# A fused tower of convolution, attention and a mixture of experts: one VectorE instruction per expert in place of two

## The chip, the cores and the metric

The kernel runs on one core of one Trainium2 chip. All data are float32. The metric is the device time of one execution in microseconds (us); before the change the median of three runs is 431.23 us (430.74 to 431.54). All numbers below are of the kernel before the change.

## What is computed

Eight samples pass one after the other through three blocks. Each has 750 frames of 64 channels; the convolution leaves 735 tokens.

```
h = conv1d(x, w_eff)                        # 16 taps, w_eff = cos(phase) w_real - sin(phase) w_imag
h = h + softmax(q k^T / 8) n                # n = layernorm(h), q = n Wq^T, k = n Wk^T, values are n
n = layernorm(h)
top two of 16 gate logits n @ gate_w + gate_b, softmax over the two
moe = sum over the chosen experts of gate * (relu(n @ w1[e] + b1[e]) @ w2[e] + b2[e])
h = h + layernorm(n + moe) * gamma + beta
```

The experts' hidden layer is 128 wide. The kernel computes all 16 experts for all tokens, and multiplies the hidden layer by a gate that is zero for experts that a token didn't choose.

## The kernel before, in words

**Tiling.** The 735 tokens are padded to 736 and lie in the free dimension, as two halves of 368 columns (HALF, line 32). A float32 matmul output of 368 columns fits in one PSUM bank; 736 don't. So each product that covers all tokens is made as two matmul groups, one for each half, into two banks.

**Streams.** Five instruction streams are written out by hand, one for each engine, with a `pipeline` that is the same for all: an opening, then passes i = 1 to 8. Pass i works on the attention of sample i, the mixture of sample i-1 (called m), the first layer norm and the score maxima of sample i+1, and the convolution of sample i+2. Passes 1 to 5 have all of these; pass 6 has no convolution; pass 7 has neither convolution nor score maxima; pass 8 is the mixture of the last sample alone (`last_mixture`). Nothing is scheduled by a tool: the order in each stream is that of the code, and semaphores tie the streams together.

**The mixture, expert by expert.** For expert e, TensorE runs `first_layer(m, e)` (L1043): for each half two matmuls, with the high and the low part of w1, into that half's bank, `up[0]` or `up[1]`. Each half's second matmul raises `s_up` by one. Then one of two ways follows:

- 13 of the 16 experts: VectorE's `hide` (L776) does bias, rectifier and gate of one half in one instruction (the larger of up and -b1, times the gate; the constant part is added by other matmuls), writes `hidden`, and raises `s_hid` by one. There are two for each expert.
- experts 10, 13 and 14 (`POOLED`, L43): ScalarE does bias and rectifier (`rectify`, L523), GpSimd the gate (`gate_hidden`, L295).

Then TensorE runs `second_layer(m, e)` (L1055), later in its stream: two matmuls that add into the bank `mix`. It waits until both halves of `hidden` are there. `hidden` has room for four experts.

**Who may write `up` again.** In passes 1 to 7 all experts use the same two banks. `first_layer` of expert e waits for each half separately until the same half of expert e-1 was read: the first half needs `s_hid` at the count that the first `hide` of e-1 gives, the second half that of the second `hide`. In pass 8 the experts rotate through three pairs of banks (`up_of`, L289: `up`, `wide0`, `wide1`) and wait for expert e-3.

**Order around the change on TensorE** (L1090 to L1190), with what stands between two first layers: 0, transposes and four score products of the attention (scores 0 and 1), 1, biases, second layer 0 and scores 2, 2, scores 3, 3, second layers 1 and 2, values and scores 4, 4, scores 5, 5, second layers 3 and 4 and values, 6, transposes of the next sample, 7, second layers 5 and 6, values and the projection, 8, three short matmuls of the attention, 9, second layers 7 and 8 and score maximum 0, 10, score maxima 1 and 2, 11, second layer 9 and a part of the convolution, 12, six transposes, 13, score maximum 3, gate logits, second layers and convolution, 14, gate transposes and score maximum 4, 15, the rest.

**Order on VectorE** (L793 to L836): the experts' `hide` pairs in order, and between them, for the next layer norm: `centre` before 0, `normalise` after 4, `keys_lo` after 7, `scale_attention` and `centre_sum` after 8, `query_lo` and `reduce_max` 0 after 9, `reduce_max` 1 and 2 before 11, `normalise` after 11, `x2_lo` and `reduce_max` 3 after 12, the top two, the gate and `reduce_max` 4 before 15.

**SyncE** sends the gates of the next sample to memory and back, as 16 broadcasts to `gates_all`, one for each expert; each waits until the expert's old gates were read (`s_hid` after both halves).

Of the kernel before, what the change touches and what calls it, by code (L numbers as in the profile page):

```python
# [25 lines left out]
ALU = mybir.AluOpType  # L26
ACT = mybir.ActivationFunctionType
# [4 lines left out]
HALF = (TOK + 1) // 2  # L32
TOKP = 2 * HALF
P = 128
# [6 lines left out]
CHUNKS = TAPS // 2  # L41
E, F = 16, 128
POOLED = (10, 13, 14)  # L43
HIDDEN = 4
CONV_CUTS = (0, 3, 5, CHUNKS)
# [3 lines left out]
BANK = 512  # L49
# [41 lines left out]
def build(nc, x_t, w_real, w_imag, phases, wq, wk, gate_w, gate_b, w1, b1_t, w2, b2, gamma, beta, out):  # L91
    ctx = ExitStack()
    with ctx:
        def sb(name, shape, dt=F32):
            return ctx.enter_context(nc.sbuf_tensor(name, shape, dt))

        def ps(name, shape):
            return ctx.enter_context(nc.psum_tensor(name, shape, F32))

        def sem(name):  # L100
            return ctx.enter_context(nc.semaphore(name))
# [16 lines left out]
        b1_neg = sb("b1_neg", [P, E])  # L118
        b1_pos = sb("b1_pos", [P, E])
# [14 lines left out]
        conv_t = sb("conv_t", [P, HALFP])  # L134
# [14 lines left out]
        x2 = [sb(f"x2_{k}", [P, TOKP + PAD], F32R) for k in range(2)]  # L149
# [10 lines left out]
        gates_all = sb("gates_all", [P, E, TOKP])  # L160
# [4 lines left out]
        relu = sb("relu", [P, 2, 2, HALF])  # L165
        hidden = sb("hidden", [P, HIDDEN, 2, HALF])
# [13 lines left out]

        wide = [ps(f"wide{k}", [P, 2, BANK]) for k in range(2)]
        small = ps("small", [P, BANK])
        up = [ps(f"up{k}", [P, BANK]) for k in range(2)]
        mix = ps("mix", [P, BANK])

        at = wide[1][:, 1, 0:2 * NT].rearrange("p (t k) -> p t k", k=2)
# [27 lines left out]
        s_ht = sem("h_transposed")  # L214
# [44 lines left out]
        s_gall = [sem(f"gates_of_expert{e}_broadcast") for e in range(E)]  # L259
        s_bmm = sem("bias_added")  # L260
        s_up = sem("up_ready")
        s_hid = sem("hidden_ready")
        s_relu = sem("relu_done")
        s_phid = sem("pooled_hidden_ready")
        s_down = sem("down_done")
# [19 lines left out]
        def split(ap):  # L285

            return ap.rearrange("p (s n) -> p s n", s=2)

        def up_of(e, tail):  # L289

            if not tail or e % 3 == 0:
                return up[0][:, 0:HALF], up[1][:, 0:HALF]
            return wide[e % 3 - 1][:, 0, 0:HALF], wide[e % 3 - 1][:, 1, 0:HALF]

        def gate_hidden(eng, n, e):  # L295

# [170 lines left out]
        def _(act):  # L467
            def copy(dst, src, scale=1.0):
                return act.activation(dst, src, ACT.Copy, scale=scale)  # L469
# [7 lines left out]
            def conv_copy(n, src=small):  # L477
                act.wait_ge(s_conv, n + 1)
                act.wait_ge(s_ht, n)
                copy(conv_t[:, 0:HALF], src[:, 0:HALF]).then_inc(s_convc, 1)  # L480
# [5 lines left out]
            def h0_copy(n, buf, src=small):  # L486
                act.wait_ge(s_ht, n + 1)
                tokens_copy(h0[buf], s_h0, src)
# [15 lines left out]
            def keys_hi_again(n):  # L504
                copy(split(keys1[0:D, :]), wide[1][0:D, :, 0:HALF]).then_inc(s_kone, 1)
# [17 lines left out]
            def rectify(n, e, tail):  # L523

                k = POOLED.index(e)
                for s in range(2):
                    act.wait_ge(s_up, 2 * E * n + 2 * e + s + 1)
                    if s == 0:
                        used = hidden_before(n, POOLED[k - 2], 1, True) if k >= 2 else hidden_before(n, e, -1, True)
                        act.wait_ge(s_phid, CREDIT + used)  # L530
                    act.activation(relu[:, k % 2, s, :], up_of(e, tail)[s], ACT.Relu, bias=b1_pos[:, e:e + 1]).then_inc(s_relu, 1)  # L531

            def exponentials(i, first, end):
                for t in range(first, end):
# [29 lines left out]
            def opening():  # L564

                shift(0)
                exponentials(0, 0, 4)
                conv_copy(1, up[0])
                exponentials(0, 4, NT)
                h0_copy(1, 1, up[1])  # L570
                variance(0, cen0[1], 1)
                attention_copy(0)
                variance(1, cen1, 0)
                keys_hi(1)
                keys_hi_again(1)
                query_hi(1)
                x2_hi(0, 0)
                exp_gap(0)
                gates_to_rows(0, False)
                conv_copy(2, up[0])  # L580
                act.wait_ge(s_h1, 1)
                h0_copy(2, 0, up[1])

            def iteration(i, par, first, att, conv, ahead):
                if att:
# [45 lines left out]
        def _(dve):  # L631
# [141 lines left out]
                dve.wait_ge(s_gate, g + 8)  # L773
                dve.tensor_tensor(gates[:], pick[:, 0, :, :], second, ALU.add).then_inc(s_gates, 1)

            def hide(n, e, s, tail):  # L776

                dve.wait_ge(s_up, 2 * E * n + 2 * e + s + 1)
                if s == 0:
                    dve.wait_ge(s_gall[e], 16 * (n + 1))  # L780
                    dve.wait_ge(s_down, HIDDEN + E * n + e - HIDDEN + 1)
                dve.scalar_tensor_tensor(hidden[:, e % HIDDEN, s, :], up_of(e, tail)[s], b1_neg[:, e:e + 1],  # L782
                                         gates_all[:, e, s * HALF:(s + 1) * HALF],
                                         ALU.max, ALU.mult).then_inc(s_hid, 1)

            def hide_both(n, e, att):
                if e not in POOLED:
                    hide(n, e, 0, not att)
                    hide(n, e, 1, not att)
                elif not att:  # L790
                    gate_hidden(dve, n, e)

# [85 lines left out]
        def _(pe):  # L878
# [6 lines left out]
            def convolve(n, par, first, end, dst=small):  # L885
                if first == 0:
                    pe.wait_ge(s_x[par], 8 * (n - par) + 16)
                for k in range(first, end):
                    for s in range(2):
                        a = s * HALF + 2 * k  # L890
                        last = mm(dst[s * D:(s + 1) * D, 0:HALF], conv_w[:, k, :], xt[par][:, a:a + HALF],
                                  k == 0, k == CHUNKS - 1)
                if end == CHUNKS:
                    last.then_inc(s_conv, 1)

            def to_tokens(src, done, dst=small):

                for j in range(BLOCKS):
                    last = pe.transpose(dst[:, j * P:(j + 1) * P], src[:, j * P:(j + 1) * P], ident[:])  # L899
                last.then_inc(done, 1)  # L900
# [142 lines left out]
            def first_layer(n, e, buf, tail=False):  # L1043

                used = e - 3 if tail else e - 1
                for s in range(2):
                    if used >= 0 and used in POOLED:
                        pe.wait_ge(s_relu, hidden_before(n, used, s, True))
                    elif used >= 0:
                        pe.wait_ge(s_hid, hidden_before(n, used, s, False))  # L1050
                    dst, rhs = up_of(e, tail)[s], x2[buf][:, s * HALF:(s + 1) * HALF]
                    mm(dst, w1_hi[:, e, :], rhs, True, False)
                    mm(dst, w1_lo[:, e, :], rhs, False, True).then_inc(s_up, 1)

# [137 lines left out]
            def opening():  # L1192


                for t in range(NT):
                    max_scores(0, t, 1 - t % 2, t - 1)
                    keep_awake(2)
                pe.wait_ge(s_moe_in, 16 * MOE_LOADS)
                transpose_max(0)
                for k in range(3):  # L1200
                    convolve(1, 1, CONV_CUTS[k], CONV_CUTS[k + 1], up[0])
                    scores(0, 2 * k)
                    scores(0, 2 * k + 1)
                pe.wait_ge(s_convc, 2)
                to_tokens(conv_t, s_ht, up[1])
                for t in range(NT):
                    weigh_values(0, t, 0)
                keep_awake(1)
                attention_to_tokens(0)
                keep_awake(2)  # L1210
                pe.wait_ge(s_attn, 1)
                keep_awake(4)
                pe.wait_ge(s_h0, 2)
                pe.wait_ge(s_ln[0], 2)
                to_features(wide[1], xn1[1], s_t1)
                keep_awake(3)
                pe.wait_ge(s_khi, 2)
                keep_awake(3)
                project(1)
                pe.wait_ge(s_ln[1], 1)  # L1220
                pe.wait_ge(s_kone, 2)
                to_features(wide[1], xn2[0], s_t2)
                convolve(2, 0, 0, 1, up[0])
                gate_logits(0, 0)
                convolve(2, 0, 1, 4, up[0])
                bias_product()
                max_scores(1, 0, 0, 0)
                transpose_gates(0)
                convolve(2, 0, 4, CHUNKS, up[0])
                pe.wait_ge(s_gtc, 1)  # L1230
                for t in range(1, NT):
                    max_scores(1, t, t % 2, t - 1)
                pe.wait_ge(s_convc, 3)
                to_tokens(conv_t, s_ht, up[1])
                pe.wait_ge(s_h0, 3)

            pipeline(pe, opening, iteration)
# [37 lines left out]
```

## Time and profile before

| | |
|---|---|
| median of three runs | 431.23 us |
| profiled execution, its own time | 430.75 us |
| its span, first to last instruction | 428.8 us |
| TensorE matmul busy | 397.3 us, 93% |
| VectorE busy | 252.4 us, 59% |
| ScalarE busy | 157.8 us, 37% |
| GpSimd busy | 129.6 us, 30% |
| mean granted TensorE clock | 0.988 of 2.4 GHz |

The profiled execution took 1.95 us more than its span; what lies around the span is the start and the end of the program. A row of the timeline or of the page counts an engine as busy from an instruction's start to its end. Matmuls overlap in their pipeline: each of 368 columns is shown for 0.33 us while the next starts 0.17 us after it. VectorE's records overlap a little too: a new instruction starts before the record of the one before it ends. "PEld" is TensorE's loading of weights, which runs ahead of its matmul; a wait of TensorE is mostly shown there. "Idle before" is time in which the engine stood still, and after it stands what released it.

### The profile page before, as it was taken

Reading aid. Unit: us, or ns where it says so; the run is one execution under the profiler, and the core shown is the slowest. Engines: PE = TensorE matmul, PEld = TensorE weight load, DVE = VectorE, ACT = ScalarE, POOL = GpSimd, SP = SyncE. Lnnn points to the kernel's source line nnn. Section 1 sums busy time; section 2 is a strip of 40 time slices with the busy share of each in tenths; the row PEclk is TensorE's granted clock in tenths of the full one; section 3 lists DMA queues with packets and bytes.
Section 4 is the critical chain, followed back from the end, with each engine's and each line's share of the span. In section 5 each row is a group of like instructions: output and inputs, shape, how many; then the busy total and the mean of one; then the engine's idle time right before and its main releaser. Section 6 shows DMA issues by size and latency. Waiting matters only on the chain.

```text
span 428.8 us, 6480 instructions
## 1 busy us (share of the span) xinstructions
PE 397.3 (93%) x2326; PEld 255.4 (60%) x2326; DVE 252.4 (59%) x607; ACT 157.8 (37%) x486; POOL 129.6 (30%) x158
## 2 busy tenths in 40 slices
PE   8889887999999999999999999999999889988892
PEld 6676554766576656666575657665666556555450
DVE  3273556458745775458545874478555964464772
ACT  1346412433263325433354335341553333232121
POOL 3100300104323442146125432244215620553601
PEclk9999969999999999999999999999999999999998
DMA  6500004910096004900194007700292019401940
GB/s 184 136 0 2 1 2 150 415 39 0 8 337 262 18 2 189 409 26 2 58 393 170 5 4 289 311 20 0 73 412 104 0 39 375 174 3 41 373 174 18
DMA packets 22847, 55.93 MB, mean 130 GB/s; under 512 B 3744, under 2 KB 4768, under 8 KB 22688
## 3 DMA queue, kind: packets, MB, share of 16 engines
q1 hardware_dynamic: 22816, 55.53, 34.4%
q8 instruction: 18, 0.29, 0.3%
q14 instruction: 13, 0.11, 0.1%
HBM read 53.57 MB, written 1.95 MB: 129 GB/s over the span
## 4 chain that ended last, share of the span: by engine, by line
PE 68%; DVE 22%; ACT 4%; issue 3%; DMA 1%; POOL 1%; POOLq 0%; SPq 0%; DVEq 0%; ACTq 0%
PE mix L880 18%; PE up L880 17%; PE wide L880 14%; PE small L880 13%; DVE row_max L720 5%; DVE hidden L782 4%; PE wide L906 3%; DVE x L659 2%; ACT x L469 1%; PE wide L1030 1%; DVE top_at L753 1%; DVE q_lo L659 1%; DVE xn L672 1%; PE wide L982 1%; PE small L899 1%
## 5 line engine op out<-in xcount | busy, mean ns | idle before, releaser
L782 DVE SCALAR_TENSOR_TENSOR hidden<-up,b_neg,gates_all 128x368 f32<-128x368 f32 x194 | 107.3, 594 | 92.8 <-PE up L880 83.6
L880 PE MATMUL mix<-hidden,w2s 128*64 128x368 f32 x512 | 94.1, 485 | 1.7 <-DVE hidden L782 1.7
L880 PE MATMUL up<-x,w_hi 128*128 128x368 f32 x236 | 87.9, 372 | 1.4 <-DVE hidden L782 0.9
L880 PE MATMUL up<-x,w_lo 128*128 128x368 f32 x236 | 77.8, 329 | 0.0
L416 POOL TENSOR_SCALAR var_eps<-var 128x6 f32<-128x6 f32 x24 | 5.8, 242 | 204.7 <-ACT cen_sq L494 204.7
L880 PEld LDWEIGHTS up<-x,w_hi 128*128 128x128 f32 x236 | 44.3, 188 | 25.0 <-issue 13.1
L880 PEld LDWEIGHTS mix<-hidden,w2s 128*64 128x64 f32 x512 | 31.0, 136 | 39.3 <-issue 27.9
L539 ACT ACTIVATE probs<-wide 128x736 f32<-128x736 f32 (+2 forms) x48 | 36.7, 785 | 42.5 <-PE wide L880 42.5
L302 POOL TENSOR_TENSOR hidden<-relu,gates_all 128x368 f32<-128x368 f32 x42 | 40.5, 984 | 39.1 <-ACT relu L531 24.8
L720 DVE TENSOR_REDUCE row_max<-wide 128x1 f32<-128x736 f32 (+1 forms) x48 | 42.2, 912 | 10.7 <-PE wide L880 10.6
L880 PEld LDWEIGHTS up<-x,w_lo 128*128 128x128 f32 x236 | 44.6, 189 | 0.0
L494 ACT ACTIVATE cen_sq<-cen 128x64 f32<-128x64 f32 x144 | 34.6, 244 | 21.6 <-DVE cen L734 16.8
L880 PE MATMUL wide<-q_hi,keys 128*128 128x368 f32 (+2 forms) x96 | 34.2, 356 | 0.2 <-ACT q_lo L469 0.2
L880 PE MATMUL small<-probs,xn 128*64 128x368 f32 (+2 forms) x192 | 33.5, 473 | 0.0
L418 POOL TENSOR_TENSOR rstd<-var_eps,power 128x6 f32<-128x6 f32 x24 | 32.4, 1351 | 2.0
L880 PE MATMUL small<-xt,conv_w 128*64 128x368 f32 x192 | 32.5, 472 | 0.0
L880 PE MATMUL wide<-q_lo,keys 65*128 65x368 f32 (+2 forms) x96 | 31.9, 333 | 0.0
L880 PE MATMUL wide<-keys,q_hi 128*128 128x368 f32 (+1 forms) x96 | 27.7, 371 | 2.7 <-DVE row_max L720 2.5
L494 ACT ACTIVATION_READ_ACCUMULATOR cen_sq<-cen 128x1 f32 x144 | 27.2, 189 | 0.0
L531 ACT ACTIVATE relu<-up,b_pos 128x368 f32<-128x368 f32 x42 | 21.5, 563 | 12.1 <-PE up L880 11.5
L880 PE MATMUL mix<-ident 128*128 128x128 f32 x138 | 21.4, 300 | 3.0 <-POOL ident L381 1.7
L880 PEld LDWEIGHTS wide<-q_hi,keys 128*128 128x128 f32 (+2 forms) x96 | 17.7, 184 | 10.7 <-issue 9.1
(136 smaller groups left out, 468.2 us busy)
## 6 DMA issues: line engine op xcount, KB each, us to landing
gates_all<-gates_far SPq DMA_DIRECT2D x128, 368.0 KB, 8.3
xt<-x_t SPq DMA_DIRECT2D x8, 375.0 KB, 12.1
out<-outs SPq DMA_DIRECT2D x8, 192.0 KB, 1.8
w_raw<-w SPq DMA_DIRECT2D x2, 512.0 KB, 6.5
w2s<-w SPq DMA_DIRECT2D x1, 512.0 KB, 7.4
gates_far<-gates_t SPq DMA_DIRECT2D x8, 46.0 KB, 1.7
gates_all<-w_real SPq DMA_DIRECT2D x1, 256.0 KB, 2.8
gates_all<-w_imag SPq DMA_DIRECT2D x1, 256.0 KB, 2.9
```

What stands on the lines that cost most here:

```text
L302: eng.tensor_tensor(hidden[:, e % HIDDEN, s, :], relu[:, POOLED.index(e) % 2, s, :], gates_all[:, e, s * HALF:(s + 1) * HALF], ALU.mult).t ...
L416: pool.tensor_scalar(var_eps[k][:], var[k][:], EPS, None, ALU.add).then_inc(s_eps[k], 1)
L418: pool.tensor_tensor(rstd[k][:], var_eps[k][:], power[:], ALU.pow).then_inc(s_rstd[k], 1)
L469: return act.activation(dst, src, ACT.Copy, scale=scale)
L494: last = act.activation(cen_sq[k][:, t, :], src[:, t, :], ACT.Square, scale=D ** -0.5, accum_out=var[k][:, t:t + 1])
L531: act.activation(relu[:, k % 2, s, :], up_of(e, tail)[s], ACT.Relu, bias=b1_pos[:, e:e + 1]).then_inc(s_relu, 1)
L539: act.activation(split(probs[0:w, t, :]), wide[t % 2][0:w, :, 0:HALF], ACT.Exp).then_inc(s_prob, 1)
L659: return dve.tensor_tensor(dst, whole, high.bitcast(F32), ALU.subtract)
L720: dve.tensor_reduce(row_max[0:w, t, D:D + 1], wide[buf][0:w, :, 0:HALF], AX.XY, ALU.max).then_inc(s_max, 1)
L782: dve.scalar_tensor_tensor(hidden[:, e % HIDDEN, s, :], up_of(e, tail)[s], b1_neg[:, e:e + 1], gates_all[:, e, s * HALF:(s + 1) * HALF], A ...
L880: return pe.matmul(dst, lhsT, rhs, start=start, stop=stop, skip_group_check=True)
L906: last = pe.transpose(dst[:, t % 2, j * P:j * P + w], src[0:w, t, 0:2 * D], ident[0:w, 0:w])
```

## The change

`up` becomes one PSUM tensor of two banks, as `wide` is. `up_of` returns one view of both halves where it returned a pair. `hide` loses its argument for the half: it is one instruction of 2 x 368 columns for each expert; it waits until `s_up` counts both halves, and raises `s_hid` by two at its end. All waits on `s_hid` keep their counts. `rectify` and `first_layer` stay as they are, for each half, with another way to name it. The copies and products of the opening that use `up` name its two banks.

```diff
-        up = [ps(f"up{k}", [P, BANK]) for k in range(2)]
+        up = ps("up", [P, 2, BANK])
...
         def up_of(e, tail):
             if not tail or e % 3 == 0:
-                return up[0][:, 0:HALF], up[1][:, 0:HALF]
-            return wide[e % 3 - 1][:, 0, 0:HALF], wide[e % 3 - 1][:, 1, 0:HALF]
+                return up[:, :, 0:HALF]
+            return wide[e % 3 - 1][:, :, 0:HALF]
...
-                    act.activation(relu[:, k % 2, s, :], up_of(e, tail)[s], ACT.Relu, bias=b1_pos[:, e:e + 1]).then_inc(s_relu, 1)
+                    act.activation(relu[:, k % 2, s, :], up_of(e, tail)[:, s, :], ACT.Relu, bias=b1_pos[:, e:e + 1]).then_inc(s_relu, 1)
...
-            def hide(n, e, s, tail):
-
-                dve.wait_ge(s_up, 2 * E * n + 2 * e + s + 1)
-                if s == 0:
-                    dve.wait_ge(s_gall[e], 16 * (n + 1))
-                    dve.wait_ge(s_down, HIDDEN + E * n + e - HIDDEN + 1)
-                dve.scalar_tensor_tensor(hidden[:, e % HIDDEN, s, :], up_of(e, tail)[s], b1_neg[:, e:e + 1],
-                                         gates_all[:, e, s * HALF:(s + 1) * HALF],
-                                         ALU.max, ALU.mult).then_inc(s_hid, 1)
+            def hide(n, e, tail):
+
+                dve.wait_ge(s_up, 2 * E * n + 2 * e + 2)
+                dve.wait_ge(s_gall[e], 16 * (n + 1))
+                dve.wait_ge(s_down, HIDDEN + E * n + e - HIDDEN + 1)
+                dve.scalar_tensor_tensor(hidden[:, e % HIDDEN, :, :], up_of(e, tail), b1_neg[:, e:e + 1],
+                                         split(gates_all[:, e, :]), ALU.max, ALU.mult).then_inc(s_hid, 2)
...
-                    hide(n, e, 0, not att)
-                    hide(n, e, 1, not att)
+                    hide(n, e, not att)
...
-                    dst, rhs = up_of(e, tail)[s], x2[buf][:, s * HALF:(s + 1) * HALF]
+                    dst, rhs = up_of(e, tail)[:, s, :], x2[buf][:, s * HALF:(s + 1) * HALF]
```

## Rows read from the trace of the kernel before

**Rows 1.** The page, busy time of the engines: us, share of the span, instructions

```profile
PE 397.3 (93%) x2326; PEld 255.4 (60%) x2326; DVE 252.4 (59%) x607; ACT 157.8 (37%) x486; POOL 129.6 (30%) x158
```

**Rows 2.** The chain of waits that ended last, its shares by line

```profile
PE 68%; DVE 22%; ACT 4%; issue 3%; DMA 1%; POOL 1%; POOLq 0%; SPq 0%; DVEq 0%; ACTq 0%
PE mix L880 18%; PE up L880 17%; PE wide L880 14%; PE small L880 13%; DVE row_max L720 5%; DVE hidden L782 4%; PE wide L906 3%; DVE x L659 2%; ACT x L469 1%; PE wide L1030 1%; DVE top_at L753 1%; DVE q_lo L659 1%; DVE xn L672 1%; PE wide L982 1%; PE small L899 1%
```

**Rows 3.** Who waited for whom, TensorE and its weight loads: us, times, longest

```profile
PE wide L880 <- DVE x L659: 6.2, 8, 1.1
...
PEld up L880 <- DVE hidden L782: 10.4, 42, 0.8
```

**Rows 4.** Timeline of TensorE in pass 4, experts 1 to 3: start, us, instruction

```profile
216.64 0.33 PE L880 MATMUL up<-x,w_hi 128*128 128x368 f32 x1
...
219.90 0.33 PE L880 MATMUL up<-x,w_lo 128*128 128x368 f32 x1
...
220.24 0.33 PE L880 MATMUL up<-x,w_lo 128*128 128x368 f32 x1
...
221.08 0.34 PE L880 MATMUL up<-x,w_hi 128*128 128x368 f32 x1
...
221.43 0.43 PE L880 MATMUL up<-x,w_hi 128*128 128x368 f32 x1
221.70 0.33 PE L880 MATMUL up<-x,w_lo 128*128 128x368 f32 x1
221.96 1.46 PE L880 MATMUL mix<-hidden,w2s 128*64 128x368 f32 x8
```

**Rows 5.** Groups of VectorE instructions by shape: busy us, mean ns, idle before

```profile
L782 DVE SCALAR_TENSOR_TENSOR hidden<-up,b_neg,gates_all 128x368 f32<-128x368 f32 x194 | 107.3, 594 | 92.8 <-PE up L880 83.6 <-issue 8.5 <-DMA gates_all<-gates_far 0.7
...
L659 DVE TENSOR_TENSOR x<-wide,x 64x736 fp32r<-64x736 f32 x8 | 7.4, 928 | 5.4 <-ACT x L469 5.4
...
L667 DVE SCALAR_TENSOR_TENSOR cen<-mean_sum,h 128x384 f32<-128x384 f32 x8 | 4.5, 558 | 0.3
```

**Rows 6.** Timeline of VectorE in pass 4, experts 0, 2, 8, 9

```profile
215.35 1.10 DVE L782 SCALAR_TENSOR_TENSOR hidden<-up,b_neg,gates_all 128x368 f32<-128x368 f32 x2
...
220.27 1.11 DVE L782 SCALAR_TENSOR_TENSOR hidden<-up,b_neg,gates_all 128x368 f32<-128x368 f32 x2 [1.98 <-PE up L880]
...
236.50 1.11 DVE L782 SCALAR_TENSOR_TENSOR hidden<-up,b_neg,gates_all 128x368 f32<-128x368 f32 x2 [2.25 <-PE up L880]
...
238.81 1.10 DVE L782 SCALAR_TENSOR_TENSOR hidden<-up,b_neg,gates_all 128x368 f32<-128x368 f32 x2
239.83 0.90 DVE L659 TENSOR_TENSOR q_lo<-wide,q_hi 64x736 fp32r<-64x736 f32 x1
240.66 2.56 DVE L720 TENSOR_REDUCE row_max<-wide 128x1 f32<-128x736 f32 x3
```

**Rows 7.** Timeline of TensorE in pass 4, after experts 9 and 10

```profile
238.19 1.46 PE L880 MATMUL mix<-hidden,w2s 128*64 128x368 f32 x8
...
241.62 0.60 PE L880 MATMUL wide<-keys,q_hi 128*128 128x368 f32 x2 [0.23 <-DVE row_max L720]
```

**Rows 8.** Timeline of TensorE in pass 4, after expert 13

```profile
247.70 0.49 PE L880 MATMUL wide<-keys,q_hi 128*128 128x368 f32 x2
248.85 0.84 PE L880 MATMUL wide<-gw,x 128*128 128x32 f32 x6 [0.66 <-DVE x L659]
```

**Rows 9.** Timeline of VectorE in passes 6 and 7, experts 0 and 11

```profile
309.86 1.11 DVE L782 SCALAR_TENSOR_TENSOR hidden<-up,b_neg,gates_all 128x368 f32<-128x368 f32 x2 [0.73 <-DMA gates_all<-gates_far]
...
380.00 1.11 DVE L782 SCALAR_TENSOR_TENSOR hidden<-up,b_neg,gates_all 128x368 f32<-128x368 f32 x2 [1.72 <-PE up L880]
381.02 1.44 DVE L672 TENSOR_TENSOR xn<-cen,rstd 128x768 f32<-128x768 f32 x1
```

**Rows 10.** Timeline of VectorE and TensorE in pass 8, experts 1 and 4

```profile
399.40 2.13 DVE L782 SCALAR_TENSOR_TENSOR hidden<-wide,b_neg,gates_all 128x368 f32<-128x368 f32 x4 [0.75 <-issue]
...
400.59 0.41 PE L880 MATMUL wide<-x,w_hi 128*128 128x368 f32 x1
```

More of the change, by code:

```diff
@@ L567, in opening @@
                 exponentials(0, 0, 4)
-                conv_copy(1, up[0])
+                conv_copy(1, up[:, 0, :])
                 exponentials(0, 4, NT)
-                h0_copy(1, 1, up[1])
+                h0_copy(1, 1, up[:, 1, :])
                 variance(0, cen0[1], 1)
@@ L579, in opening @@
                 gates_to_rows(0, False)
-                conv_copy(2, up[0])
+                conv_copy(2, up[:, 0, :])
                 act.wait_ge(s_h1, 1)
-                h0_copy(2, 0, up[1])
+                h0_copy(2, 0, up[:, 1, :])
             def iteration(i, par, first, att, conv, ahead):
@@ L1200, in opening @@
                 for k in range(3):
-                    convolve(1, 1, CONV_CUTS[k], CONV_CUTS[k + 1], up[0])
+                    convolve(1, 1, CONV_CUTS[k], CONV_CUTS[k + 1], up[:, 0, :])
                     scores(0, 2 * k)
@@ L1204, in opening @@
                 pe.wait_ge(s_convc, 2)
-                to_tokens(conv_t, s_ht, up[1])
+                to_tokens(conv_t, s_ht, up[:, 1, :])
                 for t in range(NT):
@@ L1222, in opening @@
                 to_features(wide[1], xn2[0], s_t2)
-                convolve(2, 0, 0, 1, up[0])
+                convolve(2, 0, 0, 1, up[:, 0, :])
                 gate_logits(0, 0)
-                convolve(2, 0, 1, 4, up[0])
+                convolve(2, 0, 1, 4, up[:, 0, :])
                 bias_product()
@@ L1228, in opening @@
                 transpose_gates(0)
-                convolve(2, 0, 4, CHUNKS, up[0])
+                convolve(2, 0, 4, CHUNKS, up[:, 0, :])
                 pe.wait_ge(s_gtc, 1)
@@ L1233, in opening @@
                 pe.wait_ge(s_convc, 3)
-                to_tokens(conv_t, s_ht, up[1])
+                to_tokens(conv_t, s_ht, up[:, 1, :])
                 pe.wait_ge(s_h0, 3)
```

## The prediction

> **What bounds the kernel now.** I read the page first, then the chain of waits, then who waited for whom, then the timelines of one middle pass. TensorE is busy for 93% of the span and VectorE for 59% [rows 1], and of the chain that ended last 68% is TensorE and 22% VectorE [rows 2]. What is to be seen: VectorE isn't short of time, and the two `hide` instructions of an expert are only 4% of the chain. Before them VectorE stood idle for 92.8 us, nearly all of it for TensorE's first layer [rows 5]. So time saved on VectorE is worth little in most places; what counts is how soon VectorE gives TensorE its banks and its hidden layer. There TensorE waits already, but shortly: its weight loads waited 42 times for `hidden` ahead of an `up` product, 10.4 us in all, and the matmuls ahead of the gate logits for the low part of x, 6.2 us in 8 times [rows 3]. 42 is six in each of seven passes: the places where `first_layer` of one expert follows closely on that of the last.
>
> **The instruction.** A half takes 594 ns; two in a row take 1.11 us from start to end [rows 5, 6], so the second starts 0.52 us after the first. The pair holds VectorE for 1.02 us (238.81 to 239.83, when the next instruction starts) [rows 6]. One instruction over 736 columns isn't in the trace for this operation. From below: subtractions over 736 columns with one operand in PSUM take 0.90 and 0.93 us [rows 5, 6], which also show that one instruction may cross two banks. From above: 1.11 us, if joining saves nothing. The nearest in kind is the subtraction of 0.93 us; against 384 columns in 0.56 us it costs (928 - 558) / 352 = 1.05 ns a column, and with the half's own fixed part I take 594 + 368 x 1.05 = 0.98 us. Its successor may start 0.08 us before its record ends (1.10 less 1.02), so it holds VectorE for 0.90 us: 0.12 us less for each of 104 experts, 12 us of VectorE in all, where VectorE is mostly idle.
>
> **What it loses.** Two things move, and both are TensorE's. The instruction can't start before the second half of `up` is there, one half's two matmuls (0.34 us) later than now; so where VectorE was idle, `hidden` is whole 0.34 + 0.98 - 1.11 = 0.21 us later. And the first bank, which is released after 0.59 us now, comes free only with the second. TensorE's next first layer waits with all four matmuls in place of the last two.
>
> *Experts 2 to 3, worked out in pass 4.* Now: the last matmul of expert 2 starts at 220.24; VectorE starts 0.37 us after the start of a half's last matmul (220.27 for 219.90); expert 3's first half starts at 221.08 without a wait, its second at 221.43, 0.05 us after the pair ended (221.38), and the second layer at 221.96 [rows 4, 6]. After: VectorE starts at 220.24 + 0.37 = 220.61 and ends at 221.59; expert 3 starts at 221.64; its matmuls follow at 0.27 (221.43 to 221.70), 0.17 and 0.17 us, and the second layer 0.26 us after the last (221.70 to 221.96): 222.51. That is **0.55 us later**, and the queue behind it on TensorE is everything. The same pattern, with four to six matmuls between two first layers, stands at 4 to 5 and at 6 to 7: 3 places in 7 passes, 21 x 0.55 = **11.6 us**. Nothing later in the pass gives it back, for VectorE waits 2.25 us for TensorE before expert 8 [rows 6]; its own chain starts late by the same amount.
>
> *Experts 8 to 9.* The same 0.55 us at first, but here VectorE sets the pace behind it: expert 8 (0.21 us later), the attention's scaling, expert 9 (0.12 us shorter, queued), the low part of q, row maxima. These start 0.21 - 0.12 = 0.09 us later; the maximum's matmuls, which came 1.39 us after 238.19, come after 240.13 and end at 240.74, so the first row maximum starts at 240.78, not 240.66: 0.12 us. TensorE waits for it at 241.62 [rows 7] and had waited before as well; of the 0.55 us only **0.12** go on. In passes 1 to 5 this makes 0.6 us; in pass 6, which has no convolution to cover, the second row maximum (0.4 us later) goes through expert 11 to the layer norm's transposes, 0.25 us; in pass 7 expert 8's 0.21 us and expert 11's 0.34 - 0.03 us (380.00 to 381.02, the norm is right behind it [rows 9]) go down the chain to the gates: 0.52 us. Together 1.4 us.
>
> *Experts 12 to 13.* 0.53 us again, at 247.70 + 0.53 = 248.23 for the next score maximum. Its matmuls end at 248.72, before the gate logits could start at 248.85: they wait 0.66 us for the low part of x now [rows 8]. Cost nothing; the cover is that wait, and with the cover gone it is 0.53 us a pass.
>
> *The other experts.* The first layers of 1, 2, 4, 6, 8, 10 and 12 come long enough after their forerunners'. The closest is 1 after 0: VectorE takes up expert 0 at 215.35, behind the centring, so it ends at 216.33, and TensorE comes at 216.64 [rows 4, 6]. 11, 14 and 15 wait for ScalarE's relu, which is left as it is. In passes 6 and 7 expert 0 waits for the gates' transfer [rows 9], not for TensorE, and expert 1 waits for expert 0: the instruction ends 0.13 us earlier, and two more matmuls (0.34 us) stand behind it. 0.21 us, twice: **0.4 us**. Of the queues moved past, SyncE's broadcasts wait for whole experts only; the last of them ends 0.12 us earlier. No instruction of GpSimd or ScalarE waits for a `hide`.
>
> *Pass 8.* Three pairs of banks: only expert 4 waits for expert 1, whose gates came late: its second half now at 400.59 [rows 10], both at 399.40 + 0.98 + 0.05 = 400.43, and 0.2 us more to the next product; the start of the pass gains 0.13 us. **0.1 us.** From there TensorE is the bound and finds `hidden` ready.
>
> **Sum:** 11.6 + 1.4 + 0.4 + 0.1 = 13.5 us on 430.75 us, the profiled execution's own time: 444.2. The median of the runs is 0.48 us above that execution, so I forecast **444.7 us**. With the instruction at 0.90 us it is 2.8 us less (21 x 0.08, and 0.08 twice a pass in VectorE's own stretch); at 1.11 us it is 4.5 us more.
>
> The Trainium skill has both sides in one section (Perfetto Trace Analysis, Optimizing Scalar/DVE Operations): grouping into larger operations helps "if the engine is saturated", and where it isn't but causes bubbles on others, "breaking up instructions may allow work to be completed sooner". It gives some 125 ns of overhead for each VectorE instruction on PSUM; my estimate from that page is 104 x 0.125 = 13 us, which would be a gain of 13 us if VectorE were the bound and is none where it is idle. The trace, with VectorE at 59%, is on the second side.
>
> **The rivals.**
>
> - *The cover is thinner than I read it.* The price is 0.55 us at 8 to 9 and 0.53 at 12 to 13 too, in six passes, because a wait of VectorE for TensorE moves with TensorE. For: both covers are chains that TensorE itself starts, a little earlier. Against: rows 7 and 8 show waits of TensorE left over. 6 x (0.43 + 0.53) = 5.8 us more: 450.5. Chance 7%.
> - *The joined instruction is no shorter than the pair*, or is carried out as two: 444.7 + 4.5 = 449. Against: the 0.93 us of the subtraction over two banks. 4%.
> - *One of the three places is absorbed* by slack that the rows don't show (a transfer, or ScalarE's pace in the exponentials): 7 x 0.55 less, 440.8. 5%.
> - *Faster.* VectorE's own stretch from expert 8 to the row maxima, and the gates' chain, are what each pass waits for, and TensorE catches up in the waits of rows 7 and 8 whatever happened before. Then experts 9, 11 and 15 give 0.12 us each and nothing is lost: 7 x 0.3 = 2 us, 429. It decides if the joined instruction ends before TensorE needs the first bank, which at 2 to 3 would take 0.98 - 0.55 = 0.43 us, less than a half takes now, or if VectorE weren't idle before expert 8. 3%.
> - *No change:* 2%, the case between these.
>
> **How the numbers follow.** The forecast has 79% and its own range is 442 to 447 (0.90 to 1.04 us for the instruction). The range of 8 in 10 takes in most of the second rival and the third: 440.5 to 449.5. About 0.2% (0.9 us) is what a measurement can tell from no change. Faster 3%, within 2%, slower 95%.
>
> **What would show it.** One `hide` group over 736 columns, some 97 times on `up`, near 0.98 us. The wait of `up` loads for `hidden` up from 10.4 us to some 25 (five places a pass at 0.6 to 0.7 us). In pass 4, 1.35 us between the starts of the first layers of experts 2 and 3 (221.08 less 219.73, one matmul ahead of 219.90 [rows 4]) grows to 1.9; the same at 4 and 6. The wait for the low part of x falls from 6.2 us. The distance from one pass to the next grows by 1.8 us, while TensorE's busy time stays at 397. I am wrong if that distance stays, if VectorE's idle time before expert 8 is gone, or if the instruction isn't near 1 us.

## The result: 15 us slower, and the profile after

The changed kernel takes 445.94 us (median of four runs, 443.76 to 447.92) against 430.99 us of the kernel before on the same chip: 1.035 times as long, with a 95% interval of 1.030 to 1.041. The profiled execution took 446.03 us, its span 444.1 us. I had forecast 444.7 us and a range of 440.5 to 449.5.

The first view is the page's busy time, which answers to [rows 1].

```profile
PE 400.9 (90%) x2326; PEld 258.6 (58%) x2326; DVE 240.5 (54%) x503; ACT 158.7 (36%) x486; POOL 129.8 (29%) x158
```

VectorE has 104 instructions fewer (607 to 503) and is busy for 11.9 us less, and the span is 15.3 us longer. TensorE has the same 2326 matmuls, and its busy time is 3.6 us higher; all else that the span gained is idle TensorE. Not all of the 3.6 us is work. In pass 4, at a granted clock of 1.00 in both kernels (the 2.4 GHz level), the windows view shows 0.44 us more, with no difference of clock (columns: window, its length, busy us and instructions of TensorE, weight loads, VectorE, ScalarE and GpSimd, granted clock, DMA share, GB/s; first before, then changed):

```profile
214.06:260.93 46.87, 45.84 (x273) 29.30 (x272) 29.59 (x72) 19.16 (x61) 17.06 (x18) 1.00 0.36 143
```
```profile
219.66:268.53 48.87, 46.28 (x273) 29.57 (x272) 28.18 (x59) 19.27 (x61) 17.02 (x18) 1.00 0.36 137
```

By the same view passes 2 to 7, all at 1.00, make 2.1 us of the 3.6. My reading: where the next matmul waits, the row of the last one counts for its whole 0.33 us, and not only for the 0.17 us until the next starts. The rest lies in the opening and in passes 1 and 8, where the stretches at half clock are (below).

The second view is the groups of instructions by shape, for the joined instruction and a subtraction over two banks; it answers to [rows 5]. Behind the bar: busy us, mean ns, idle before it and what ended that.

```profile
L781 DVE SCALAR_TENSOR_TENSOR hidden<-up,b_neg,gates_all 128x736 f32<-128x736 f32 x97 | 95.2, 981 | 120.7 <-PE up L877 89.7 <-issue 22.1 <-DMA gates_all<-gates_far 8.9
...
L659 DVE TENSOR_TENSOR x<-wide,x 64x736 fp32r<-64x736 f32 x8 | 7.4, 928 | 3.7 <-ACT x L469 3.7
```

The joined instruction takes 0.981 us, where the two took 1.11 from start to end. VectorE's idle time before it grew from 92.8 to 120.7 us: what was saved became waiting, and more came on top.

The third view is who waited for whom on TensorE and its weight loads: us in total, times, longest. It answers to [rows 3].

```profile
PE up L877 <- DVE hidden L781: 19.1, 39, 1.1
PE wide L877 <- DVE x L659: 1.8, 3, 1.1
...
PEld up L877 <- DVE hidden L781: 31.0, 41, 1.4
```

The weight loads' wait ahead of the first layer is 31.0 us where it was 10.4, in as many places, and TensorE itself now stands still there for 19.1 us. The wait for the low part of x fell from 6.2 to 1.8 us: that is the cover at experts 12 to 13 being used.

The fourth view is the timeline of TensorE in pass 4 around experts 2 and 3, the place worked out in the prediction; it answers to [rows 4].

```profile
225.32 0.34 PE L877 MATMUL up<-x,w_hi 128*128 128x368 f32 x1
...
225.84 0.33 PE L877 MATMUL up<-x,w_lo 128*128 128x368 f32 x1
...
227.30 0.44 PE L877 MATMUL up<-x,w_hi 128*128 128x368 f32 x1 [0.45 <-DVE hidden L781]
227.57 0.33 PE L877 MATMUL up<-x,w_lo 128*128 128x368 f32 x1
227.74 0.33 PE L877 MATMUL up<-x,w_hi 128*128 128x368 f32 x1
227.92 0.33 PE L877 MATMUL up<-x,w_lo 128*128 128x368 f32 x1
228.18 1.46 PE L877 MATMUL mix<-hidden,w2s 128*64 128x368 f32 x8
```

And the fifth is VectorE's timeline there and in its own stretch at experts 8 and 9; it answers to [rows 6].

```profile
226.26 0.98 DVE L781 SCALAR_TENSOR_TENSOR hidden<-up,b_neg,gates_all 128x736 f32<-128x736 f32 x1 [2.11 <-PE up L877]
...
244.31 0.98 DVE L781 SCALAR_TENSOR_TENSOR hidden<-up,b_neg,gates_all 128x736 f32<-128x736 f32 x1 [2.23 <-issue]
...
246.50 0.98 DVE L781 SCALAR_TENSOR_TENSOR hidden<-up,b_neg,gates_all 128x736 f32<-128x736 f32 x1
247.39 0.90 DVE L659 TENSOR_TENSOR q_lo<-wide,q_hi 64x736 fp32r<-64x736 f32 x1
```

The last matmul of expert 2 starts at 225.84. VectorE starts at 226.26 and ends at 227.24; expert 3 starts 0.06 us later, all four of its matmuls behind the wait. From the start of expert 2's first layer to the second layer it is now 228.18 - 225.32 = 2.86 us; it was 221.96 - 219.72 = 2.24 (219.72 is the start of the matmul ahead of 219.90 in [rows 4], by the same timeline). That is 0.62 us at one place.

**The passes.** The clearest measure of a kernel here is the distance between the same matmul in two passes, since passes 2 to 5 are alike and ran at a granted clock of 1.00, the 2.4 GHz level, in all the profiles. In the changed kernel the first matmul of expert 0 starts here in passes 2 and 6 (timeline of TensorE):

```profile
121.97 0.41 PE L877 MATMUL up<-x,w_hi 128*128 128x368 f32 x1
...
317.38 0.42 PE L877 MATMUL up<-x,w_hi 128*128 128x368 f32 x1
```

(317.38 - 121.97) / 4 = 48.85 us a pass. In the kernel before the two rows are

```profile
120.36 0.42 PE L880 MATMUL up<-x,w_hi 128*128 128x368 f32 x1
...
307.76 0.42 PE L880 MATMUL up<-x,w_hi 128*128 128x368 f32 x1
```

which gives 46.85 us. So a pass is **2.00 us longer**; I had reckoned 3 x 0.55 + 0.12 = 1.77. By the same rows, expert by expert in pass 4, the distance between the starts of two first layers grew by 0.62 us at 2 to 3, 0.63 at 4 to 5, and 0.74 at 6 to 7, of which 0.14 came back by expert 8; at 8 to 9 it grew by 0.72, and 0.11 and 0.42 came back by 10 and 11, so that 0.19 stayed; at 12 to 13 it grew by 0.73 and 0.73 came back by 14. The other distances changed by 0.03 us or less.

**The clock.** The kernel's single runs differ by 4 us, and it is the granted clock that they differ by: 443.76 us at 0.995, 445.86 at 0.984, 446.03 at 0.983, 447.92 at 0.977. In the profiled run the windows view shows one such stretch in pass 8, at half clock, the 1.2 GHz level, beside one at the 2.4 GHz level (columns as above):

```profile
412.30:415.70 3.40, 3.03 (x9) 1.90 (x10) 2.19 (x3) 0.00 (x0) 3.08 (x4) 0.51 0.98 393
415.80:432.00 16.20, 16.20 (x90) 9.78 (x91) 10.62 (x14) 2.88 (x6) 3.27 (x4) 1.00 0.65 257
```

Ahead of the first, TensorE had stood still for 1.56 us, for a VectorE instruction that waited for the gates' transfer; inside it the `up` matmuls follow at 0.30 us by the timeline, not 0.17. Leaving out the last microseconds of each program, where TensorE has no work, such stretches of 3.4 us or twice that stand in the profiles of all kernels here but `both_late`, at changing places: in that of before 6.8 us in the opening (56.8 to 63.6), in that of the changed kernel 3.4 us in the opening, 3.4 us around the start of pass 1 and the one in pass 8. None lies in passes 2 to 5. In the changed kernel's profile the one at pass 1 cost 0.3 us (49.2 against 48.86) and the one in pass 8 1.1 us (see the part on pass 8). They come without the change too, so the passes decide below where the medians are 1 or 2 us off.

### The profile page after: what moved, and what is told of

The parts are those of the page before. It is cut to its first block and busy times, and to the rows that moved or that the text cites. A ratio compares the mean times of both kernels' runs of the same rounds, so it can differ in the third digit from the quotient of the medians.

```text
span 444.1 us, 6480 instructions
## 1 busy us (share of the span) xinstructions
PE 400.9 (90%) x2326; PEld 258.6 (58%) x2326; DVE 240.5 (54%) x503; ACT 158.7 (36%) x486; POOL 129.8 (29%) x158
## 5 line engine op out<-in xcount | busy, mean ns | idle before, releaser
L781 DVE SCALAR_TENSOR_TENSOR hidden<-up,b_neg,gates_all 128x736 f32<-128x736 f32 x97 | 95.2, 981 | 120.7 <-PE up L877 89.7
L877 PE MATMUL up<-x,w_hi 128*128 128x368 f32 x236 | 86.6, 367 | 19.5 <-DVE hidden L781 19.1
```

What stands on the lines that cost most here:

```text
L781: dve.scalar_tensor_tensor(hidden[:, e % HIDDEN, :, :], up_of(e, tail), b1_neg[:, e:e + 1], split(gates_all[:, e, :]), ALU.max, ALU.mult). ...
L877: return pe.matmul(dst, lhsT, rhs, start=start, stop=stop, skip_group_check=True)
```

## The experiments

The same measure for all, and their medians (before, beside them on the chip, 430.4 to 431.0 us):

| kernel | us a pass | against before | median us |
|---|---|---|---|
| before | 46.85 | | 430.99 |
| changed | 48.85 | +2.00 | 445.94 |
| release_late | 47.87 | +1.02 | 440.1 |
| start_late | 48.20 | +1.35 | 440.8 |
| both_late | 49.31 | +2.46 | 449.2 |
| split246 | 47.05 | +0.20 | 434.7 |
| split_close | 46.73 | -0.12 | 431.5 |
| cover | 47.91 | +1.06 | 439.7 |
| up_last | 49.06 | +2.21 | 446.9 |
| wait_udg | 48.86 | +2.01 | 446.7 |
| wait_ug | 48.85 | +2.00 | 445.8 |
| join_911 | 46.74 | -0.11 | 429.4 |
| join_911_ug | 46.73 | -0.12 | 429.4 |

### The change taken apart: what each of its waits costs alone

`release_late` has the two instructions of before, and only TensorE's wait is as late as in the change:

```diff
-                        pe.wait_ge(s_hid, hidden_before(n, used, s, False))
+                        pe.wait_ge(s_hid, hidden_before(n, used, 1, False))
```

> The kernel before (two instructions per expert), but TensorE's first half of the next expert also waits for the second instruction. Theory (bank release): where first layers follow closely, all four matmuls stand behind the wait in place of two, 0.34 us more at experts 2 to 3, 4 to 5 and 6 to 7 of seven passes, and 8 to 9 and 12 to 13 stay covered: 21 x 0.34 = 7.1 us, 438 us. Rival (late hidden layer: what costs is that the hidden layer is whole later): VectorE's times don't change, so 431 us.

It took 1.023 times as long as before (1.018 to 1.028), 440.1 us with single runs from 438.1 (clock 0.987) to 442.5 (0.976). The pass grew by 1.02 us, which is 3 x 0.34. TensorE around experts 2 and 3, by its timeline:

```profile
221.14 0.33 PE L880 MATMUL up<-x,w_lo 128*128 128x368 f32 x1
...
221.48 0.33 PE L880 MATMUL up<-x,w_lo 128*128 128x368 f32 x1
...
222.68 0.43 PE L880 MATMUL up<-x,w_hi 128*128 128x368 f32 x1 [0.18 <-DVE hidden L782]
222.95 0.33 PE L880 MATMUL up<-x,w_lo 128*128 128x368 f32 x1
```

and VectorE's pair by its own:

```profile
221.51 1.11 DVE L782 SCALAR_TENSOR_TENSOR hidden<-up,b_neg,gates_all 128x368 f32<-128x368 f32 x2 [1.98 <-PE up L880]
```

VectorE is as it was: it starts at 221.51, 0.37 us after the start of the first half's second matmul (221.14), and ends at 222.62. The hidden layer of the closely followed expert isn't a bit later; TensorE's four matmuls behind 222.62, in place of two, are the whole loss. So the rival that looks at the hidden layer alone is out.

`start_late` is the other half: VectorE waits for both halves of `up`, each half is released by itself.

```diff
-                dve.wait_ge(s_up, 2 * E * n + 2 * e + s + 1)
+                dve.wait_ge(s_up, 2 * E * n + 2 * e + 2)
```

> The kernel before, but VectorE's first instruction of an expert waits for both halves of up; each half is still released by itself. Theory: the pair ends 0.34 to 0.39 us later, so 21 x 0.37 = 7.8 us at the three close places, and about 0.37 us a pass through expert 8 and VectorE's own stretch, 2.6 us: 441 us. Rival (late hidden layer alone): all of the loss of the change and more, since the pair also takes 0.13 us longer than the joined instruction: 446 us or above.

1.021 times (1.016 to 1.026), 440.8 us, 1.35 us a pass. My reckoning of 0.37 us at three places and once more through expert 8 would be 1.48 us; expert by expert in pass 4 it is 0.34, 0.33, 0.33 and 0.35. Again less than the change, as the theory has it. The rows for experts 1 and 2, the last `up` matmul and the pair of VectorE behind it:

```profile
222.16 0.33 PE L880 MATMUL up<-x,w_lo 128*128 128x368 f32 x1
...
225.25 0.33 PE L880 MATMUL up<-x,w_lo 128*128 128x368 f32 x1
```
```profile
222.53 1.11 DVE L782 SCALAR_TENSOR_TENSOR hidden<-up,b_neg,gates_all 128x368 f32<-128x368 f32 x2 [1.05 <-PE up L880]
...
225.62 1.11 DVE L782 SCALAR_TENSOR_TENSOR hidden<-up,b_neg,gates_all 128x368 f32<-128x368 f32 x2 [1.98 <-PE up L880]
```

The pair starts 0.37 us after the start of the matmul that it waits for, now the second half's.

`both_late` has both edits.

> The kernel before with both of the above: the joined instruction's waits, with two instructions. Theory: the two prices add, 431 + 7 + 10 = 448 to 449 us, and the change is this less what joining saves, 0.13 us at 21 places and once or twice a pass in VectorE's stretch, 3 to 4 us: 445 to 446 us. Rival (the joined instruction itself does harm, in reading two banks or in the clock): this kernel is faster than the changed one.

1.044 times (1.038 to 1.049), 449.2 us, 2.46 us a pass, where the two alone make 1.02 + 1.35 = 2.37: they add, but for 0.09 us. This kernel has the waits of the changed one and differs from it only by the joining. Joining is thus worth 2.46 - 2.00 = 0.46 us a pass. It doesn't do harm by itself: it is the only gain in the change.

### The change kept, but not where first layers follow closely

`split246` and `split_close` are the changed kernel with two instructions again for experts 2, 4 and 6, and for 2, 4, 6, 8 and 12 (`hide_half` is the old `hide`):

```diff
-                if e not in POOLED:
+                if e not in POOLED and e in (2, 4, 6, 8, 12):
+                    hide_half(n, e, 0, not att)
+                    hide_half(n, e, 1, not att)
+                elif e not in POOLED:
                     hide(n, e, not att)
```

> The changed kernel, but experts 2, 4, 6, 8 and 12 (whose first layer is followed closely by the next one) have two instructions again; experts 0, 1, 3, 5, 7, 9, 11 and 15 keep one. Theory: the whole loss was at these five: 430 to 431 us, perhaps 0.12 us a pass below the kernel before through expert 9. Rival (joined instructions cost everywhere, by a later hidden layer): 8 of 13 joined leave half the loss or more, 438 us or above.

The ratio is 0.9997 (0.997 to 1.002), 431.5 us. Joining eight of thirteen experts costs nothing, and the pass is 0.12 us shorter than before: expert 9's gain. All of the loss lay at the five places. The new way to lay out and name `up`, which this kernel has too, costs nothing either.

> The changed kernel with two instructions again for experts 2, 4 and 6 alone; 8 and 12 keep one. Theory: the three open places give back all but what goes through expert 8: 21 x 0.61 us = 12.8 us of the changed kernel's 445.9, so 433 us, and pass by pass some 0.2 us over the kernel before. Rival (the covers at 8 to 9 and 12 to 13 are thin): those cost 0.4 to 0.5 us each in six passes, 437 to 438 us.

1.012 times (1.006 to 1.018), 434.7 us, and 0.20 us a pass. The three open places carried 48.85 - 47.05 = 1.80 us of the pass's 2.00; the 0.20 that are left are 0.32 for experts 8 and 12 joined (47.05 - 46.73, the two kernels differ by them alone) less the 0.12 of expert 9, where the rival wanted 0.8 to 1. The median is 1.7 us above my 433: one of the four runs took 438.7 us at a clock of 0.970, and the two fastest 433.4 and 433.7.

### The wait covered in place of removed

`cover` has all instructions joined and another order on TensorE, at three places like this one:

```diff
                 scores(i, 3)
-                first_layer(m, 3, buf)
                 second_layer(m, 1)
+                first_layer(m, 3, buf)
                 second_layer(m, 2)
```

> The changed kernel with all instructions joined, but TensorE's order altered: second layer 1 stands between first layers 2 and 3, second layer 3 between 4 and 5, second layer 5 between 6 and 7. Same work; some 0.7 us of it now stands in front of each wait, and each move costs about 0.2 us in changes between shapes. Theory: the wait is covered, 21 x (0.61 - 0.2) = 8.6 us less than the changed kernel, 437 us. Rival (the loss lies in the joined instruction, or in VectorE): 446 us or more, since nothing of VectorE changes.

1.021 times (1.016 to 1.026), 439.7 us: 6.3 us less than the changed kernel, where I expected 8.6. TensorE at experts 2 and 3 in pass 4:

```profile
222.60 0.34 PE L877 MATMUL up<-x,w_hi 128*128 128x368 f32 x1
...
223.79 0.34 PE L877 MATMUL wide<-q_lo,keys 65*128 65x368 f32 x1
224.06 0.84 PE L877 MATMUL mix<-hidden,w2s 128*64 128x368 f32 x4
224.83 0.44 PE L877 MATMUL up<-x,w_hi 128*128 128x368 f32 x1
```

There is no wait left: VectorE's joined instruction starts at 223.54 by its timeline and is done at 224.52, before TensorE comes. The place costs 0.23 us more than before. I put that down to the two changes of shape, which no other run tests: 0.27 us from scores to `mix` and 0.31 us from the last `mix` matmul (224.06 + 3 x 0.155 = 224.52) back to `up`, where matmuls of one shape follow at 0.17 and 0.155. At experts 4 to 5 it is 0.23 us and at 6 to 7 0.39, by the same timeline, and the last is what I had too low. The loss is a wait that other work can fill; this filling is dearer than two instructions on an idle VectorE.

### How soon the joined instruction starts

It starts 0.42 us after the start of the last `up` matmul (226.26 for 225.84 above), the halves 0.37 us. Three kernels looked for the cause in its three waits. `up_last` puts the wait for `up` last; `wait_udg` has up, second layer, gates; `wait_ug` leaves out the wait for the second layer, which TensorE's order implies.

> The changed kernel with the joined instruction's three waits in another order: gates and second layer first, up last. In the changed kernel it starts 0.42 us after the start of the last up matmul, where I had reckoned with 0.37. If the two further waits stand behind up and cost the 0.05 us: about 1.4 us less, 444.5 us, and the distance is 0.37 us in the trace. If they don't: 445.9 us and 0.42 us.

> The changed kernel with the joined instruction's waits in the order up, second layer, gates, in place of up, gates, second layer. In the built program the first half's instruction of the kernel before has its waits in the order second layer, gates, up, and starts 0.37 us after the last matmul's start; the joined one has gates, second layer, up and 0.42 us; with up first in the code's last place (up_last) second layer, up, gates and 0.47 us. This kernel's built order is that of the kernel before. Theory (the order of the built waits sets the distance): 0.37 us, the pass from 48.86 to 48.65 us, 444.5 us. Rival (the joined shape takes 0.05 us longer to start): 0.42 us and 48.86 us.

> The changed kernel without the joined instruction's wait for the second layer, which TensorE's order implies (the up matmuls of expert e stand behind the second layer of expert e-4). If each wait beside up costs 0.05 us: 0.37 us from the last matmul's start, the pass 48.65 us, 444.5 us. If the wait isn't what costs: 0.42 us and no change.

`up_last` went the other way: its joined instruction in pass 4 starts at 227.96 for a matmul at 227.50, 0.46 us (at the other places 0.46 to 0.48),

```profile
227.96 0.98 DVE L781 SCALAR_TENSOR_TENSOR hidden<-up,b_neg,gates_all 128x736 f32<-128x736 f32 x1 [2.11 <-PE up L877]
```

and the pass is 0.21 us longer than the changed kernel's. `wait_udg` and `wait_ug` kept 0.42 us and 48.85 us a pass. So the two other waits cost nothing as long as the one for `up` stands first in the code, and 0.04 to 0.05 us when it stands last. My idea of where the 0.05 us come from fell. `start_late`, with three waits and the same late signal, starts at 0.37 us; what is left is the joined shape itself, but that is only argued: no run has two banks and half the columns.

### Joined only where it pays

`join_911` is the kernel before with one instruction for experts 9 and 11 (built from the changed kernel, with `hide_half` twice for all others).

> The kernel before with one instruction for experts 9 and 11 alone, which VectorE takes up from its queue with both halves of up long there. Theory: nothing is lost, and VectorE's stretch that TensorE waits for gets 0.12 us shorter in each pass: 430 to 430.5 us, against 431. Rival: no gain, since the row maximum behind it waits for TensorE's matmuls: 431 us.

The ratio is **0.9967 (0.994 to 0.9994)**, 429.4 us against 430.4: faster than both kernels, though the interval comes within 0.06% of no change, so that the passes below are the firmer sign. VectorE in pass 4:

```profile
238.07 0.56 DVE L734 TENSOR_TENSOR cen<-attn,cen 128x384 f32<-128x384 f32 x1
238.54 0.98 DVE L781 SCALAR_TENSOR_TENSOR hidden<-up,b_neg,gates_all 128x736 f32<-128x736 f32 x1
239.44 0.90 DVE L659 TENSOR_TENSOR q_lo<-wide,q_hi 64x736 fp32r<-64x736 f32 x1
240.27 2.56 DVE L720 TENSOR_REDUCE row_max<-wide 128x1 f32<-128x736 f32 x3
```

The joined instruction holds VectorE for 0.90 us, not 1.02 as in [rows 6], with no wait before or after it. The row maxima come 0.12 us sooner, and the pass is 0.11 us shorter. Expert by expert all of it shows between experts 10 and 11, so it is expert 9's; in passes 2 to 5 expert 11's joining gave nothing that can be seen.

`join_911_ug` takes the wait for the second layer away as well.

> The kernel before with one instruction for experts 9 and 11 alone, and without the wait for the second layer ahead of VectorE's first instruction. Theory: as before with 9 and 11 joined, 46.73 us a pass, and up to 0.05 us less at the places where TensorE waits for a second half (6 to 7, and at times 2 to 3 and 4 to 5): 46.6 to 46.7 us a pass, 428.5 to 429.5 us. Rival: the wait for the second layer costs nothing, 46.73 us.

46.73 us a pass, 429.4 us, 0.998 times (0.995 to 1.0005): the halves start at 0.37 us with that wait or without. It costs nothing. The pass is again 0.12 us shorter than before, though these runs alone would not tell it.

## Why the prediction was right

**The instruction.** 0.98 us taken, 0.981 measured. That the gain is no more than the second instruction's fixed part holds, and `both_late` shows its worth, 0.46 us a pass.

**Experts 2 to 3, 4 to 5, 6 to 7.** The mechanism is as described, and `release_late` and `start_late` show its two parts. The size was 0.55 us a place; 0.60 to 0.63 were measured. The mis-sized part is the start: 0.42 us after the last matmul, where I took the halves' 0.37. Over 21 places this is 1.1 us.

**Experts 8 to 9.** "Of the 0.55 us only 0.12 go on" was 0.19. The same late start is in it (0.05 us).

**Experts 12 to 13.** Free, as said, but 0.73 us were lost and regained where I had 0.53, more than the 0.66 us of TensorE's wait for the low part of x that I took for the whole cover. It was thicker: the weight loads ahead of the gate logits waited longer than the matmuls, 0.96 us before, and they still wait 0.37 us in the changed kernel.

```profile
248.85 0.74 PEld L880 LDWEIGHTS wide<-gw,x 128*128 128x128 f32 x6 [0.96 <-DVE x L659]
```
```profile
256.45 0.74 PEld L877 LDWEIGHTS wide<-gw,x 128*128 128x128 f32 x6 [0.37 <-DVE x L659]
```

**Passes 6 and 7.** Predicted 1.65 + 0.21 + 0.25 = 2.1 us and 1.65 + 0.21 + 0.52 = 2.4 us. Their first layers' starts, by TensorE's timeline, lie 44.39 and 41.52 us apart before, and 46.47 and 43.89 after: 2.1 and 2.4 us. That the sums agree so well is luck. Expert by expert the three places took 1.80 and 1.84 us, expert 0 only 0.05 and 0.17 where I had 0.21, and experts 8 to 15 0.24 and 0.36 where I had 0.25 and 0.52. The term of expert 0 can't be read from two profiles at all: it hangs on when the gates' transfer lands, and with experts 0 and 1 as before `join_911` has it 0.47 and 0.39 us lower. In `wait_ug`, at the full clock, pass 7 took 44.77 us.

**Pass 8.** Predicted 0.1 us, and in this profile it took 1.2 us more (its start moved by 14.07 us, the span by 15.28), with the stretch at half clock in it. `wait_ug`, which differs from the changed kernel by one wait that costs nothing, has no such stretch there: from the first matmul of pass 8 to the end its profile shows 35.3 us, where that of before has 35.2 and that of the changed kernel 36.4. So the 0.1 us stand, as well as one profile can tell, and what the sum lacked is the clock. The opening was 0.7 us shorter, so the sum is 2.0 x 4 + 2.1 + 2.4 + 2.3 (pass 1, with another such stretch) + 1.2 - 0.7 = 15.3 us, against 13.5. With pass 1 at 2.0, pass 8 at 0.1 and the opening as before it would be 14.6: of the 1.8 us that I was short, 1.1 lie in the passes, most of it the late start, and 0.7 in the clock.

**The rivals.** *Thinner cover* is out by `split246` (0.32 us a pass for experts 8 and 12 together, 0.20 with expert 9's gain). *No shorter than the pair* is out by 981 ns. *One place absorbed*: none was. *Faster* needed VectorE's gain without TensorE's loss; that is `join_911`, and it gave the 0.12 us a pass that I had reckoned for expert 9. The section of the Trainium skill weighed in the prediction (Perfetto Trace Analysis, Optimizing Scalar/DVE Operations) has both halves shown here: where VectorE works through a queue, a larger operation helped (expert 9, 0.12 us a pass), and where it stands idle but TensorE waits for it, smaller ones let work be "completed sooner" (2.00 us a pass).

**What would show it.** The wait of the `up` loads went to 31 us where I said some 25 (I had misread the 42 waits of before as six in each pass: by place, 32 are the second halves of experts 3, 5, 7, 9 and 13, and the other ten lie in passes 6 to 8), the distance from expert 2 to 3 to 1.98 us where I said 1.9, and VectorE's idle time before expert 8 stayed (2.23 us). TensorE's busy time went up by 3.6 us where I said none: 2.1 us of it in passes 2 to 7 at the full clock, the rest in the opening and passes 1 and 8, with the stretches at half clock.

## What to carry to other kernels

Two instructions on two banks are not waste when a matmul stream refills the first bank while the second is read: count the work that the stream has between the two uses, and join only where that is longer than the last matmul's lag, the whole instruction and the hand-back together (here 0.42 + 0.98 + 0.06 us after the start of the last matmul). An engine at 59% with its idle time right before the instruction gains nothing by a shorter total. Join where it works through a queue and others wait for the end of that queue: of thirteen experts that is number 9 here. The kernel with 9 and 11 joined was 0.3% faster than the one before.

## What the runs showed of the hardware that I had not expected

The joined instruction of 2 x 368 columns starts 0.42 us after the last matmul's start and the single half 0.37 us, and leaving out a further wait changed neither. The order of waits in the code mattered once: with the wait that comes last in time also last in the code the start was at 0.46 to 0.48 us, and a pass 0.21 us longer. And stretches of 3.4 us at half the clock stand at other places in the profile of one kernel than in that of the next, where the change between them can't be the reason (`wait_ug` has none in pass 8, the changed kernel one). The changed kernel's four runs spread over 4 us, and the lower their mean clock, the longer they took: 443.8 us at 0.995, 447.9 at 0.977.
